# Attention values copied out by one ScalarE instruction and set on the block diagonal by four DMAs

## What is computed

```python
x = _ln(jnp.transpose(msa, (0, 3, 2, 1)), ln_m_g, ln_m_b)     # (1, 256, 32, 64): l, n, d
q = heads(x @ Wq); k = heads(x @ Wk); v = heads(x @ Wv)       # 8 heads of 8
g = jax.nn.sigmoid(heads(x @ Wg + bg))
scores = jnp.einsum('blhnd,blhmd->blhnm', q, k) / sqrt_c + bias
w = jax.nn.softmax(scores, axis=-1)                           # 32 x 32 for each l and head
attn = g * jnp.einsum('blhnm,blhmd->blhnd', w, v)
out = attn @ Wo + bo
```

## Time and profile before

| | us |
|---|---|
| median of 3 runs (381.38 to 383.0) | 381.95 |
| the profiled execution | 382.4 |
| its span, from the first to the last instruction | 380.6 |

### The profile page before, as it was taken

How to read it: one execution, slowest core, us unless ns; L and a number is a source line. 1 busy time by engine, 2 the same in 40 slices (tenths; PEclk the granted TensorE clock), 3 DMA queues, 4 the chain that set the end, 5 groups by cost and what they waited for, 6 DMA issues and landing times.

```text
span 380.6 us, 11216 instructions
## 1 busy us (share of the span) xinstructions
PE 306.0 (80%) x3934; PEld 195.2 (51%) x3935; DVE 285.0 (75%) x570; ACT 198.0 (52%) x333; POOL 209.8 (55%) x182
## 2 busy tenths in 40 slices
PE   0596859798777659344989999999999999999970
PEld 0296425455445333112456666666666666666640
DVE  3888776989999987788377777777777777777750
ACT  0177788989999743720034444444444444444430
POOL 2732214788888892558315555555555656555431
PEclk9988965989999989956899999999999999999995
DMA  7350102454554472796403333433333333333421
GB/s 187 65 170 0 59 0 59 140 167 143 193 169 139 162 213 61 214 272 251 152 16 56 57 55 58 60 62 56 66 58 54 57 55 55 55 56 57 58 37 14
DMA packets 25419, 36.71 MB, mean 96 GB/s; under 512 B 4560, under 2 KB 18000, under 8 KB 24624
## 3 DMA queue, kind: packets, MB, share of 16 engines
q1 hardware_dynamic: 17136, 26.00, 22.1%
q0 software_dynamic: 7488, 10.23, 17.1%
q10 hardware_dynamic: 768, 0.14, 0.3%
HBM read 25.35 MB, written 9.44 MB: 91 GB/s over the span
## 4 chain that ended last, share of the span: by engine, by line
PE 55%; ACT 11%; DVE 10%; issue 7%; POOL 6%; DMA 6%; POOLq 1%; ACTq 0%; SPq 0%; DVEq 0%
PE bank L835 23%; PE bank L858 11%; PE bank L846 4%; ACT kq L1004 3%; PE bank L659 3%; PE bank L568 3%; DVE maxes L1266 2%; PE bank L532 2%; PE bank L823 2%; POOL v_t L484 2%; PE bank L742 2%; DMA out_dram<-w_stage,gate 2%; ACT v_t L975 2%; DMA token_rows<-z_stack 2%; DVE s_exp L1275 2%
## 5 line engine op out<-in xcount | busy, mean ns | idle before, releaser
L835 PE MATMUL bank<-w_exp,w_stage 128*128 x468 | 113.7, 379 | 0.2 <-DVE w_stage L1467 0.2
L514 POOL DMA_INDIRECT out_dram<-w_stage,gate x39 | 61.8, 1585 | 76.0 <-ACT w_stage L1101 73.2
L835 PEld LDWEIGHTS bank<-w_exp,w_stage 128*128 128x128 f16 x468 | 45.6, 97 | 39.5 <-issue 1.1
L858 PE MATMUL bank<-w_exp,kq 128*128 x468 | 57.8, 273 | 1.0 <-ACT kq L1093 1.0
L1101 ACT ACTIVATE w_stage<-w_stage,gate 128x256 f32<-128x256 f32 x39 | 19.8, 508 | 62.4 <-DVE w_stage L1499 62.4
L1477 DVE TENSOR_TENSOR v_t<-bank,x_rows 128x512 f32<-128x512 f32 x39 | 27.0, 692 | 32.3 <-PE bank L835 32.2
L858 PEld LDWEIGHTS bank<-w_exp,kq 128*128 128x128 f16 x468 | 45.4, 98 | 6.9 <-issue 1.2
L500 POOL DMA_INDIRECT w_stage<-token_rows,gate x39 | 38.7, 992 | 18.4 <-PE bank L823 14.7
L414 POOL TENSOR_TENSOR w_exp<-w_stage,w_exp 128x1024 f16<-128x1024 f32 x16 | 34.1, 2135 | 12.2 <-ACT w_exp L1015 12.2
L1093 ACT ACTIVATE kq<-bank 128x512 f16<-128x512 f32 x39 | 23.3, 597 | 23.8 <-PE bank L846 23.8
L1082 ACT ACTIVATE w_stage<-bank 128x256 f16<-128x256 f32 x39 | 15.0, 384 | 39.8 <-PE bank L823 39.8
(11 more groups left out here) (249 smaller groups left out, 556.6 us busy)
## 6 DMA issues: line engine op xcount, KB each, us to landing
w_stage<-in_L_ffn_gate_w_dram SPq DMA_DIRECT2D x8, 512.0 KB, 3.9
w_stage<-in_L_ffn_up_w_dram SPq DMA_DIRECT2D x8, 512.0 KB, 3.5
w_stage<-in_L_ffn_down_w_dram SPq DMA_DIRECT2D x8, 512.0 KB, 3.5
x_rows<-in_x_dram SPq DMA_DIRECT2D x8, 256.0 KB, 6.4
out_dram<-x_rows SPq DMA_DIRECT2D x4, 512.0 KB, 6.1
token_rows<-z_stack SPq DMA_DIRECT2D x4, 512.0 KB, 6.0
x_rows<-in_L_ffn_gate_b_dram SPq DMA_DIRECT2D x1, 2048.0 KB, 11.7
z_stack<-in_L_ffn_up_b_dram SPq DMA_DIRECT2D x2, 1024.0 KB, 6.8
```

The source lines that it names most:

```text
L514: pool.indirect_dma_start(out, bass.IndirectOffsetOnAxis(t_scatter[:, b:b + 1], 0), yw[b % 2], None, compute_op=ALU.add).then_inc(s[f"y_la ...
L835: mm = pe.matmul(GU[par][k][:], xs[par][:, c, :], w_exp[:, w * W_EXP + k * W_PIECE + c * FF:][:, bass.ds(e, FF)], start=(n == 0), stop=(n ...
L858: mm = pe.matmul(YB[:, 0:L_COL], hs[par][:, c, :], w_exp[:, w * W_EXP + 2 * W_PIECE + c * L_COL:][:, bass.ds(e, L_COL)], start=(n == 0), s ...
```

## The change

`values_out(j)` becomes one instruction over all 128 rows. It writes a new plain buffer `v_row` (128 x 512, channel outermost, t and head innermost), signals `v_copied`, and waits before it, instead of for PE's `attend`, for the DMAs that have emptied `v_row` of step j-1 (`v_in`). A new function `place_values(j)` on SP issues four DMAs, one for each row group u, 32 partitions by 2 KB each, from `v_row` into the block u of `v_tile[j % 2]`. That buffer's order becomes block, channel, t and head, so that a DMA writes a contiguous run in each partition and the 36 columns of an `attend` matmul lie 64 elements apart. `attend(j, 0)` waits for `v_in`, and `project` for `v_copied`. The small buffer `rden` moves into space of another tile to make room, and the memsets of the ones follow the new order.

```diff
+            def place_values(j):
+
+                if j == 0:
+                    sp.wait_ge(s["ones_ready"], N_ONES)
+                if j >= 2:
+                    sp.wait_ge(s["av_ps"], 2 * (j - 1))
+                sp.wait_ge(s["v_copied"], j + 1)
+                for u in range(GROUP):
+                    rows = slice(32 * u, 32 * u + 32)
+                    sp.dma_start(v_tile[j % 2][rows, u, 0:D_HEAD, :],
+                                 v_row[rows, :].rearrange("p (c t) -> p c t", c=D_HEAD)).then_inc(s["v_in"], 16)
+
             load_weights(0)
...
             copy_tokens(3)
+            place_values(0)
             for j in range(PAIRS - 1):
                 if j >= 1 and j + 3 < PAIRS:
                     copy_tokens(j + 3)
                 load_weights(j + 1)
+                place_values(j + 1)
...
-                    pe.wait_ge(s["v_ready"], GROUP * j)
+                    pe.wait_ge(s["v_copied"], j)
...
                 if c == 0:
-                    pe.wait_ge(s["v_ready"], GROUP * (j + 1))
+                    pe.wait_ge(s["v_in"], 16 * GROUP * (j + 1))
...
-                                       v_tile[par][:, 4 * c + q, h, :, :], start=True, stop=True)
+                                       v_tile[par][:, :, :, HEADS * (4 * c + q) + h], start=True, stop=True)
...
                 act.wait_ge(s["v_ps"], j + 1)
-                if j == 0:
-                    act.wait_ge(s["ones_ready"], N_ONES)
-                if j >= 2:
-                    act.wait_ge(s["av_ps"], 2 * (j - 1))
-                for u in range(GROUP):
-                    rows = slice(32 * u, 32 * u + 32)
-                    act.activation(v_tile[j % 2][rows, :, :, u, 0:D_HEAD],
-                                   bank[4][rows, :].rearrange("p (t h c) -> p t h c", t=8, h=HEADS),
-                                   ACT.Copy).then_inc(s["v_ready"], 1)
+                if j >= 1:
+                    act.wait_ge(s["v_in"], 16 * GROUP * j)
+                act.activation(v_row[:].rearrange("p (c t) -> p c t", c=D_HEAD),
+                               bank[4].rearrange("p (t c) -> p c t", c=D_HEAD), ACT.Copy).then_inc(s["v_copied"], 1)
```

More of the change, by code:

```diff
@@ L92, in build @@
         maxes = sb("maxes", [P, 2, 2 * CHUNK])
-        rden = sb("rden", [P, 2, 32])
+        v_row = sb("v_row", [P, TOK])
         wo_half2 = sb("wo_half2", [P, 2, D_MODEL])
@@ L140, in build @@
         g_col, b_col, bo_col, bg_col, qb_col, kb_col, vb_col, gb_col = (small[:, 144 + i:145 + i] for i in range(8))
-        v_tile = [v_t[:, i, :].rearrange("p (t h b c) -> p t h b c", t=8, h=HEADS, b=GROUP) for i in range(2)]
+        v_tile = [v_t[:, i, :].rearrange("p (b c t) -> p b c t", b=GROUP, c=VCOL) for i in range(2)]
+        rden = tok_s[:, 0, 0:2, :]
         N_TABLES = 11
@@ L241, in build @@
             q_ps k_ps v_ps g_ps s_ps av_ps at_ps wo_ps
-            q_ready k_ready max_ready sub_ready exp_ready et_ready v_ready
+            q_ready k_ready max_ready sub_ready exp_ready et_ready v_copied v_in
             rden_ready norm_ready gate_ready gate_one gated_ready x1_ready w_hi_done w_hi_pool w_lo_done
@@ L377, in _ @@
                 for u in range(4):
-                    ones(pool.memset(t[32 * u:32 * u + 32, :, :, u, D_HEAD], 1.0))
+                    ones(pool.memset(t[32 * u:32 * u + 32, u, D_HEAD, :], 1.0))
             pool.wait_ge(s["pair_v"], 1)
```

## The result

| | us |
|---|---|
| before, median of 4 runs | 381.66 |
| with the change, median of 4 runs (428.11 to 430.76) | 429.3 |
| profiled execution with the change; its span | 430.76; 428.9 |

The ratio is 1.125, with a 95% interval of 1.1217 to 1.1284. The forecast was 437, in a range of 417 to 455.

A forecast was written before the change was run, and what follows sets the result against it. ACT (10.20 us) and DVE (9.62) nearly fill a 10.3 us step; the change closes a loop of 6.82 + 7.64 + 4.6 = 19.1 us. 382.4 + 57.0 - 1.9 = 437.5, predicted 437 us, range 417 to 455.

The forecast's parts named there:

- Placement behind the third load, the loop: SP's queue: placement waits behind POOL's last weight piece, closing a loop through PE, ACT, POOL and SP; 19.1 us a step.
- PE's part at the low clock, 6.82 us: PE, from the start of `attend(j,0)` to the end of the gates: 6.82 us at the low clock, 4.15 at full.
- ACT, POOL, SP's wake-up, 7.64 us: From the end of the gates through tanh and POOL's gate and weight pieces to SP's third load: 7.64 us.
- From the third load to `attend`, 4.6 us: SP and DMAs: third load's issue to the fourth placement's landing, queued behind 512 KB, 4.55, plus PE's wake-up: 4.6 us.
- The sum: Whole kernel: `attend(1,0)` at 75.3, six steps of 19.1, `attend(7,0)` at 189.9, 57.0 later; 437.5 us profiled, 437 predicted.
- the case that I forecast: Attention steps at the low clock without stride penalty, placement landing 3.7 to 6.0 us: 431 to 447 us, chance 0.55.
- the early or full clock: PE's clock returns within the scores or does not fall; 16.4 us a step at full clock, 421 us; 415 to 430, chance 0.22.
- At the end, 1.9 us back: After `attend(7,0)`: last softmax already done, so attends and normalisations take 4.0 us, not 5.9; routing and experts untouched.
- The new eviction, 0.69 us and off the path: ACT's single eviction takes 0.69 us, at most 2.58, and runs hidden under PE's scores.
- The new layout of the ones changes addresses, not instructions: Memsets of the ones and `rden`: the new layout was listed among the edits that cost nothing.
- The strided read: PE's `attend` slowed by columns 256 B apart: 443 us if twice as long, 453 if four times; 443 to 465, chance 0.18.
- The hidden placement at 377 to 382 us: Placement leaves right after the eviction and lands in time; ACT relieved, DVE binds, at most 0.7 us a step gained; chance 0.03.

The follow-up runs named there:

- e1: The changed kernel with the placement of step j+1 issued ahead of its three weight loads; 378.75 us, ratio 0.9878 to the kernel before.
- e2: The changed kernel with the placement issued between the second and the third weight load; 411.91 us, ratio 1.0744 to the kernel before.
- e5: The changed kernel with the placement issued between the first and the second weight load; 380.57 us, ratio 0.9954 to the kernel before.
- e7: The changed kernel with 26 dummy matmuls on PE ahead of attend's wait for the placement; 420.66 us, ratio 1.102 to the kernel before.
- e6: The changed kernel with two plain buffers, so ACT's eviction waits for the placement of two steps before; 429.35 us, ratio 1.1238 to the kernel before.

## Why the prediction was right, point by point

- **Placement behind the third load, the loop:** right, shown by the chain of waits above and by e1, e2 and e5, which take it out, shorten it and open it.
- **PE's part at the low clock, 6.82 us:** 117.25 - 110.86 = 6.39 in the step shown, and 6.2 on average over the six steps. One of them, of 6.79, is as long as step 0's part; in the others the clock comes back before the gates are done, and the shortest takes 5.5. e7 shows what the low clock costs.
- **ACT, POOL, SP's wake-up, 7.64 us:** from 117.25 to the third load at 124.89 it is 7.64, and 7.64 to 7.66 in all six.
- **From the third load to `attend`, 4.6 us:** 129.76 - 124.89 = 4.87 in the step shown and 4.8 on average, but made otherwise than the text has it. I let the placement queue behind the 512 KB. The chain shows 0.89 us until the first of four issues, three issues of 0.6 each, and 2.12 from the last one to its landing, which is what a small DMA took alone. No queueing of this last one behind the load shows. The time is SP's issues and the latency of one DMA. The mechanism of this term was wrong, and that its size fits is luck.
- **The sum:** `attend(1,0)` at 73.17 instead of 75.3. The first `attend` came at 53.73, 3.3 us earlier than before and not 1, but 2.1 of them were there when the first eviction started, at 44.3 instead of 46.4 (the first start in the line of L975 above, and in this one):

```profile
L986 ACT ACTIVATE v_row<-bank x8: 597/600/602, 44.3 to 165.5; 128x512 f32<-128x512 f32 x8
```

  From there to the `attend` it is 1.2 us less, which is about the 1 that I took. Of the 2.1, half of one can be the memsets. The rest may be chance of the one execution profiled: e1, e2, e5, e6 and e7 begin with the same program and have the first `attend` at 54.3 to 55.7. Six steps of 18.67 instead of 19.1 make 185.21 instead of 189.9. These are the 5 us by which the step from 382.4 was oversized, and the end gave back 2.0 more than I had. So the measured 429.3 lies below the 431 to 447 of the case that I forecast and inside the 415 to 430 of the early or full clock: the loop was right, and its sum a little too long.
- **At the end, 1.9 us back:** 3.3 by the end of the attention's last add, and otherwise; 0.6 more came back in the routing and the experts. DVE in order of time after the change:

```profile
189.99 0.42 DVE L1307 TENSOR_TENSOR att_n<-bank,tok_s 128x256 f32<-128x256 f32 x1
...
190.52 0.17 DVE L1353 COPY maxes<-small 128x16 f32<-128x16 f32 x1
...
196.96 0.75 DVE L1324 SCALAR_TENSOR_TENSOR x_rows<-bank,small,x_rows 128x512 f32<-128x512 f32 x1
```

  and the last two of these instructions before:

```profile
138.93 1.42 DVE L1343 COPY maxes<-small 128x16 f32<-128x16 f32 x1
...
147.95 0.75 DVE L1314 SCALAR_TENSOR_TENSOR x_rows<-bank,small,x_rows 128x512 f32<-128x512 f32 x1
```

  From `attend(7,0)` to the end of the last normalisation it took 5.2 us, not 4.0, because two transposes of the router stand between the two attends on PE. From there to the end of the last add, 7.3 us against 9.9: a copy of 0.17 instead of 1.42 us, and behind it the router's first matmuls on PE, 1.04 instead of 1.91 us. I had left this stretch unchanged.
- **The new eviction, 0.69 us and off the path:** 0.60, off the path.
- **"The new layout of the ones changes addresses, not instructions":** wrong, by 0.48 us; the eight memsets became shorter.
- **The rivals.** The clock at full speed in the loop: it did not happen for a whole step, and e7 gives 420.66 us for it, where 421 had been worked out. That the two agree is luck: e7's step takes 17.1 us and not 16.4, and what follows `attend(7,0)` is 3.1 us shorter than in the sum (whose 2.4 at the end should be 2.7 by its own terms). The strided read: it costs 0.05 us a step in the loop (1.24 against 1.19 us at the low clock), and more only at the full clock (below). The hidden placement at 377 to 382 us: e1 is that case, at 378.75, but not for the reason given, since ACT was relieved there and the steps were no shorter.

## What to carry to other kernels

A DMA that is added to a queue waits for everything that the issuing engine waits for ahead of it. Before adding one, list the waits in front of it in that queue, follow each back, and see whether one hangs on the very work that the DMA feeds: then the step becomes as long as the way round. If so, try its place in the queue before giving up the change; here two lines in another order were worth 50 us. And a large wait that the profile puts on one engine need not be on the loop: e6 removed 22.4 us of it and gained nothing.

## What the runs showed of the hardware

- `attend`'s 64 records, with a moving operand of 36 float32 columns that lie 256 B apart, take 1.22 us at the full clock and 1.24 to 1.25 at the low one; with columns side by side 0.77 and 1.19. In these rows the strided read does not get faster with the clock. At the full clock they agree with the Trainium skill's rule on strides ("SBUF — State Buffer", the part on the DMA port swizzle), with a price of 0.45 us a call; at the low one the price is 0.05.
- A ScalarE copy of 32x512 from PSUM that reads with a stride of 8 elements and writes side by side took 0.589 us; reading side by side and writing runs of 8 with gaps, 0.642. Over 128 partitions, in the first of these two orders, it took 0.600.
- A 64 KB DMA of 32 partitions inside the SBUF landed in 2.0 to 3.6 us, median 2.5, behind the weight load, and in 1.9 to 3.5, median 2.0, with the token copy ahead of it (e1). Its issue took SP 0.52 to 0.59 us in the step shown.
